# Earlier statistics pieces, an earlier third weight chunk, and low halves made by GpSimd in the first token group of a two-layer transformer block

## What is computed

```
x = x + L0_ffn(L0_cond(x))      # 64x64 matrix per sequence; 1024x1024 matmul plus gated LoRA
x = x + L1_ffn(L1_cond(x))      # one of 8 1024x1024 matrices per sequence; then:
def _bitlinear(x, w):
    scale = jnp.mean(jnp.abs(w))
    q = jnp.round(jnp.clip(w / (scale + EPS), -1.0, 1.0))
    return x @ (q * scale).T
inter = _bitlinear(h, w_gate) * _bitlinear(h, w_up)     # inner width 2752
out = _bitlinear(inter, w_down)
```

## Time and profile before

| what | value |
|---|---|
| runs shown | 1397.62 us median of three (1390.33, 1397.62, 1397.9) |
| profiled execution, its own time | 1390.51 us |
| its span, first to last instruction | 1388.9 us |
| TensorE busy | 1328.1 us (96% of the span) |
| VectorE, ScalarE, GpSimd busy | 727.2, 409.2, 141.8 us |
| mean granted TensorE clock | 0.992 of 2.4 GHz |

### The profile page before, as it was taken

The page is one execution under the profiler, slowest core; times in us unless marked ns, Lnnn a source line. Parts: engine busy times, 40 slices in busy tenths (PEclk is TensorE's granted clock), DMA queues, the critical chain, the costliest instruction groups (busy, mean ns, idle before and its releaser), DMA issues.

```text
span 1388.9 us, 23462 instructions
## 1 busy us (share of the span) xinstructions
PE 1328.1 (96%) x8864; PEld 847.3 (61%) x8864; DVE 727.2 (52%) x1187; ACT 409.2 (29%) x456; POOL 141.8 (10%) x79
## 2 busy tenths in 40 slices
PE   6999999979999979999999999999999999999998
PEld 5556655435555544555444788844888844888843
DVE  5456666434553337888854355572455581455521
ACT  3345442222332327777720011110111110111100
POOL 3200000000000000000000133210133310232200
PEclk9999999989999999999999999999999999999999
DMA  9899992999949229999683644445633354544354
GB/s 244 274 384 345 355 334 54 286 309 322 204 188 233 71 69 335 335 335 334 217 293 139 227 152 159 148 185 173 221 134 140 143 217 177 191 159 159 137 186 144
DMA packets 171949, 302.48 MB, mean 218 GB/s; under 512 B 99008, under 2 KB 131008, under 8 KB 164064
## 3 DMA queue, kind: packets, MB, share of 16 engines
q1 hardware_dynamic: 158496, 260.00, 56.6%
q10 hardware_dynamic: 12352, 40.90, 8.3%
q0 software_dynamic: 1024, 0.53, 0.2%
HBM read 212.39 MB, written 68.03 MB: 202 GB/s over the span
## 4 chain that ended last, share of the span: by engine, by line
PE 70%; DVE 7%; DMA 7%; issue 6%; SPq 5%; ACT 4%; POOL 1%; ACTq 0%; POOLq 0%; DVEq 0%
PE pair L962 26%; PE pair L999 14%; PE pair L761 10%; PE pair L843 10%; DMA wb_scratch<-region_q 3%; DMA region_q<-wb_scratch 2%; ACT region_q L1181 2%; SPq L519 2%; PE pair L676 2%; PE pair L729 2%; PE pair L744 2%; PE pair L898 1%; DVE region_q L1614 1%; PE pair L779 1%; SPq L503 1%
## 5 line engine op out<-in xcount | busy, mean ns | idle before, releaser
L962 PE MATMUL pair<-act_t,region_q 128*128 128x256 f16 x3696 | 404.0, 273 | 0.7 <-DMA region_q<-wa_scratch 0.7
L962 PEld LDWEIGHTS pair<-act_t,region_q 128*128 128x128 f16 x3696 | 361.6, 98 | 43.4 <-DMA region_q<-wa_scratch 1.2
L999 PE MATMUL pair<-region_q,region_w 128*128 128x512 f16 x1232 | 267.6, 379 | 6.3 <-DMA region_q<-wb_scratch 5.9
L661 POOL TENSOR_TENSOR region_w<-region_q,region_w 128x1792 f32 (+1 forms) x33 | 118.4, 3588 | 1149.9 <-ACT region_w L1206 1149.9
L999 PEld LDWEIGHTS pair<-region_q,region_w 128*128 128x128 f16 x1232 | 120.0, 98 | 152.8 <-DMA region_q<-wb_scratch 7.9
L843 PE MATMUL pair<-region_w,act_t 128*128 x816 | 182.4, 380 | 3.4 <-issue 1.9
L761 PE MATMUL pair<-region_w,act_t 128*128 128x512 f16 x768 | 169.0, 380 | 0.0
L898 PE MATMUL pair<-act_t,region_q 128*128 128x512 f16 x704 | 156.0, 380 | 0.0
L1212 ACT ACTIVATE region_q<-pair 128x512 f32<-128x512 f32 x33 | 19.7, 597 | 403.1 <-PE pair L962 403.1
L843 PEld LDWEIGHTS pair<-region_w,act_t 128*128 x816 | 79.9, 98 | 94.5 <-issue 6.1
L1303 DVE SCALAR_TENSOR_TENSOR act_t<-pair,act_t 128x512 f32 (+1 forms) x66 | 61.1, 947 | 133.3 <-ACT act_t L1031 133.3
(11 more groups left out here) (187 smaller groups left out, 1026.6 us busy)
## 6 DMA issues: line engine op xcount, KB each, us to landing
region_q<-wa_scratch SPq DMA_DIRECT2D x33, 1792.0 KB, 7.4
region_q<-wb_scratch SPq DMA_DIRECT2D x28, 1408.0 KB, 6.1
region_q<-in_L_cond_weight SPq DMA_DIRECT2D x40, 512.0 KB, 8.2
w1s_scratch<-region_q ACTq DMA_DIRECT2D x40, 512.0 KB, 6.0
wa_scratch<-region_q SPq DMA_DIRECT2D x22, 896.0 KB, 5.9
region_w<-in_L_ffn_w_gate SPq DMA_DIRECT2D x16, 688.0 KB, 8.9
wb_scratch<-region_q SPq DMA_DIRECT2D x11, 896.0 KB, 4.1
region_q<-in_L_ffn_w_gate SPq DMA_DIRECT2D x19, 512.0 KB, 5.1
```

What stands on the lines that cost most here:

```text
L661: pool.tensor_tensor(at(iop[:, 1], u), st[s][:, 0:7], at(iop[:, 0], u), ALU.subtract)\
L962: mm = pe.matmul(bank(s_bank, b)[:, (1 - h) * HALF:(2 - h) * HALF], ring_a[s][:, h, o_a, k], moving[a], start=(opens and h == 1 and k == 0 ...
L999: mm = pe.matmul(bank(s_bank, b), iop[:, a, p, o_a, tp * P:(tp + 1) * P], ring_b[r][:, p], start=(opens and p == 0 and a == 0), stop=(not ...
```

## The change

It has three parts. (a) Pieces 4 and 5 are issued by SP right behind pieces 0 to 3, ahead of the wait for the end of stage 1 and of rank 1; pieces 8 and 9 are summed one pair later. (b) The third chunk (n = 2) is clipped, rounded and two thirds transposed between the last pairs of stage 2, before `gate_up(0)`; its kind 2 now shares bank 6 and is transposed before `gate_up(1)`; `turn_b(0)` and `turn_a(1)` on DVE come ahead of the first product. (c) The low halves of the first group go from DVE to POOL, with the same semaphores.

```diff
-PIECES_AT = {0: range(0, 4), 1: range(4, 6), 2: range(6, 10), 3: range(10, 12), 5: range(12, 18), 9: range(18, 24)}
+PIECES_AT = {0: range(0, 4), 1: range(4, 6), 2: range(6, 8), 3: range(8, 12), 5: range(12, 18), 9: range(18, 24)}
...
-            return bank16((6, 7, 6 if isinstance(ic, int) and ic < 2 else 4)[kind])
+            return bank16((6, 7, 6 if isinstance(ic, int) and ic < 3 else 4)[kind])
...
             for p in range(4):
                 load_piece(sp, p)
+            sp.wait_ge(tmpw_transposed, 2)
+            for p in range(4, 6):
+                load_piece(sp, p)
             sp.wait_ge(main_done, NT)
...
                 if r == 1:
-                    sp.wait_ge(tmpw_transposed, 2)
-                    for p in range(4, 12):
+                    for p in range(6, 12):
                         load_piece(sp, p)
...
-            for g in range(1, NG):
+            for g in range(NG):
                 with pool.Fori(0, NP // 2) as i:
...
-                    if isinstance(n, int) and n < 2 and kind == 2:
+                    if isinstance(n, int) and n < 3 and kind == 2:
                         pe.wait_ge(q_out[0], n + 1)
-                    elif isinstance(n, int) and 0 < n <= 2 and kind == 0:
+                    elif isinstance(n, int) and 0 < n <= 3 and kind == 0:
                         pe.wait_ge(q_out[2], n)
...
             linear_t(k - 2, 1)
+            turn_q(2, 0, 1, (0, 1))
             pe.wait_ge(z_low, GRP // SEQ)
             gate_up(0, 0)
...
+            turn_q(2, 0, 1, (2,))
+            gate_up(1, 1)
             pe.wait_ge(slots_done, 1)
-            turn_q(2, 0, 1)
-            gate_up(1, 1)
...
             high_z(k - 3)
+            round_q(2, 0, 1)
             copy_z(k - 1, 0)
...
-            round_q(2, 0, 1)
...
-                store_q(m + 1, (m + 1) % 2, (m + 1) // 2)
+                store_q(m + 1, (m + 1) % 2, (m + 1) // 2, (0, 1, 2) if m == 1 else (2, 0, 1))
...
             low_z(k - 3)
+            quantize(2, 0, 1)
             copy_z(k - 1, 0)
             low_z(k - 2)
+            turn_b(0)
+            turn_a(1, 1)
             product(0, 0, 0, 0)
...
-            for m in range(4):
+            for m in range(1, 4):
                 if m > 1:
                     product(m - 1, (m - 1) % 2, (m - 1) // 2, (m - 1) // 2 % 2)
-                if m == 3:
-                    low_inter(0, 0)
                 quantize(m + 2, m % 2, m // 2 + 1)
...
-                    if c % 2 == 1:
-                        low_inter(2 * i + (c - 3) // 2, (c - 3) // 2 % 2)
...
-            low_inter(NP - 1, (NP - 1) % 2)
             down(0)
```

More of the change, by code:

```diff
@@ L1627, in turn_b @@
                 v.tensor_tensor(wd[:, 6], wd[:, 1], wd[:, 4], ALU.subtract).then_inc(wb_ready, 1)
-            def low_inter(u, s):
-                v.wait_ge(inter_high, u + 1)
-                v.tensor_tensor(at(iop[:, 1], u), st[s][:, 0:7], at(iop[:, 0], u), ALU.subtract).then_inc(inter_low, 1)
             def turn_a(n, h):
@@ L1820, in _ @@
                 product(m - 1, (m - 1) % 2, (m - 1) // 2, (m - 1) // 2 % 2)
-                if m % 2 == 1:
-                    low_inter((m - 3) // 2, (m - 3) // 2 % 2)
                 if m < IC - 2:
```

## The result

The changed kernel takes 1399.74 us (median of 20 executions, 1394.24 to 1408.58), the kernel before 1393.40 (20 executions, 1386.12 to 1397.90). The ratio is 1.0056, with a 95% interval of 1.004 to 1.0071: slower by 0.56%, some 8 us by the ratio and 6 by the medians. I had named 1385 and a range to 1395, so the forecast had the wrong sign and the range does not hold the result.

What follows compares the result with a forecast made beforehand. TensorE, busy 96% of the span, was taken as the bound. -5.9 - 6.7 + 2.5 = -10.1 us gave 1380.4 from the profiled 1390.5, or 1387.5 from the median 1397.6; 1385 was named, range 1372 to 1395.

Steps and rivals of the forecast that it cites:

- Part (a), -5.9: Stage 2: the 9.05 us stall at 288 us goes, about 3 us return at pair 5; -5.9 us, bounds -10 and -3.
- the gap of 4 to 4.5 us is filled; piece 17 then lands that much earlier: DMA queue near 308.5 to 312.5 us: asking for rank 2 earlier fills the idle gap, so piece 17 lands 4 to 4.5 us earlier.
- The slack of 1.5 us: Pair 5 after piece 17 landed: 0.8 us spare on DVE and 0.7 on PE, counted into the 5.9 us gain.
- My third rival: The pieces' stall moves to pairs 2 and 5, leaving only 3 us; sum -7.2, time 1388, chance 0.13.
- Part (b), -6.7: Third chunk around `gate_up(0)` and `gate_up(1)`: the stage moves 6.7 us earlier; bounds -7.9 and -3.
- PE stands still for 2.6 us: Between `gate_up(0)` and `gate_up(1)`: PE waits 2.6 us until ACT has emptied bank 6.
- Part (c), loop, +0.4: Loop over chunk pairs: POOL's low half holding a DVE step costs 0.4 us in all over eight or nine pairs.
- the three clips behind it: Loop, DVE: with `turn_a`'s last step held until 631, these end about 634, making ACT 0 to 0.15 us late.
- the fourth rival: POOL's low half falls on the loop's round trip: 3.3 us a pair, 29.7 over nine; sum +19, time 1414, chance 0.07.
- Part (c), `down(0)`, +1.4: `down(0)`: the last low half ends later on POOL, delaying the third product's weights; +1.4 us, bounds 0 and 2.
- "Slower": Whole kernel over 1% slower: chance 0.07, from POOL's low half falling on the loop's round trip.
- The second rival: Loop: the low half does bind, so freeing DVE gains 7.8 us more; sum -17.5, time 1378, chance 0.06.

Runs made afterwards that it cites:

- e1: Part (a) alone on the kernel before: 1391.79 us, ratio 0.9998.
- e2: Part (b) alone on the kernel before: 1390.82 us, ratio 0.9990.
- e3: Part (c) alone on the kernel before: 1406.26 us, ratio 1.0094.
- e5: Kernel before plus part (c), with SyncE's loads of the next even chunk ahead of the odd chunk's store: 1398.00 us, ratio 1.0048.
- e6: Kernel before plus part (c), with GpSimd's low half also waiting for VectorE's next product: 1393.86 us, ratio 1.0027.
- e9: Kernel before plus parts (a) and (b), ScalarE's store moved up, TensorE's three optional pairs removed: 1383.07 us, ratio 0.9935 to the kernel before.
- e4: Kernel before plus parts (a) and (b), without (c): 1388.98 us, ratio 0.9975.

## Why the prediction was wrong, point by point

- **Part (a), -5.9.** The place (pair 5) and the cause (piece 17 behind rank 2) were right. The step that failed is "the gap of 4 to 4.5 us is filled; piece 17 then lands that much earlier". The gap was filled, but by transfers at 92 GB/s; piece 17 was summed at 350.84 in e1 against 352.07 before, 1.2 us earlier, and the wait handed back was 9.05 us instead of 3. The slack of 1.5 us was also that of one execution: in e2, e3, e5 and e6, whose code is the same up to there, TensorE waits 2.81, 1.22, 2.18 and 1.12 us at this place. The term is 0. My third rival, a stall that moves, had this mechanism, with 3 us left by its estimate.
- **Part (b), -6.7.** Measured -2.4 (and -1.8 in e2, from its own marks). The step that failed is "PE stands still for 2.6 us"; it measured 5.16. I counted the waits for ScalarE alone, at the lengths that its steps had in the old place: the bank empty 3.5 us after `gate_up(0)`. I removed a stall of 6.92 us without asking what else lay under it or what the change moves into the stretch. TensorE was through its own jumps 5.9 us after `gate_up(0)` (the term that I did not have), and ScalarE's store, behind reads that took 1.8 us longer, was done after 5.5. The lower clock behind such a wait came with it: 8.57 us for `gate_up(1)`, where I had 7.0. With ScalarE's store moved up and without the jumps (e9) the stretch from the mean to `gate_up(2)` is 68.83 us, 7.5 below before: what I counted on is there, but not in this kernel.
- **Part (c), loop, +0.4.** The hold itself was foreseen, with its 3.7 us and its place, the last step of `turn_a`. The step that failed is the list of what is late behind it: "the three clips behind it". I followed VectorE's own list, and not SyncE's, where the store of that step's result has the next loads behind it. Measured +8.7 with the last chunk. It is not the fourth rival either: that had the low half on the round trip in every pair at 3.3 us, and its price of 29.7 us; what happened is 2 us in every second pair, through a queue.
- **Part (c), `down(0)`, +1.4.** Right: +1.2, with the 0.98 us wait of TensorE in the third product.
- **The rule on the shared ports.** The Trainium skill, page "SBUF — State Buffer", section "Who interferes with whom", says that operations of the clip's kind can enter a mode that takes the shared ports, and that the one issued first holds them. e6 agrees with both: clips of 4.08 us, and a GpSimd step of 3.95 behind a clip. I gave the rule no effect on the sum, and in the changed kernel, where GpSimd is done before the clips start, it had none.
- **The chances.** "Slower" had one mechanism with 0.07. All three terms that failed erred to the same side: in (a) and (b) I named the wait that goes and not the next one that lay under it, in (c) the step that is held and not the list that waits for it. The second rival's sum is -17.9 by its own terms, not -17.5; no chance hangs on the difference.

## What to carry to other kernels

Before a stall is credited as a gain, list everything that finishes inside it: another transfer in the same queue, or the engine's own jump over skipped code, may be nearly as long and is shown as the stall's cause only once the first is gone. Add what the change itself moves into that stretch. When an instruction may be held, follow every list that waits for its result, the DMA issuer's first, since there a wait also stops the transfers queued behind it. A gate that is fed by a shared queue is opened together with the next gate on that queue, or not at all: two edits worth 0 and some 3 us alone gave about 10 together.

## What the runs showed of the hardware that I had not expected

- The long jump over skipped code cost TensorE 2.7 to 3.2 us in the six kernels without part (b), where the DMA engines were nearly idle at that moment (share 0.02), and 6.1 to 6.7 us in the seven that have it and the jump, where they were busy (1.01 to 1.02); the shortest jump here is 0.22. In all thirteen the trace has one instruction transfer of 16 KB that begins inside the jump and takes 0.9 to 1.1 us, and the jump ends 1.5 us behind it. What differs is when the transfer begins: 0.3 to 0.8 us into the jump, or 3.7 to 4.3. The Trainium skill, page "Runtime: NRT & Kernel Launch", section "Instruction fetch mechanics", says that a taken branch whose target is not at hand must fetch its code first; the long jumps agree with it. Whether the traffic or the new place of the code delays the transfer is open, since no run changes one alone.
- A VectorE clip with a single tensor operand is held by GpSimd (0.81 to 4.08 us) just as the two-operand steps are (0.42 to 3.75), and GpSimd is held in turn (3.58 to 3.95).
- Two transposing transfers asked for behind a full queue took 31 to 39 us (31.06 in e4, 33.34 in e1, 39.18 in the changed kernel), and 20 to 24 us asked for 11 us later at an empty one (before, e2, e3). But for the changed kernel's (339.5) they end at about the same time, 330.4 to 334.1 us.
